# Moving the edge counting of a four-layer graph network into its two attention passes, the sort to the front, and the running maxima beside the dense products

## The reference, cut to what matters

```python
edge_index = jnp.stack([src, dst])
x = _layernorm(x + _L0_gnn_ref(x, edge_index, edge_attr, ...))  # MLP on [x[src], edge_attr], mean by dst
x = _layernorm(x + _L1_gnn_ref(x, edge_index, ...))             # two attention convolutions, 4 heads, then 1
x = _layernorm(x + _L2_gnn_ref(x, src, dst, ...))               # three SAGE convolutions
x = _layernorm(x + _L3_gnn_ref(x, edge_attr, ..., src, dst))    # softmax over edges by dst of x[src] + edge_attr

def sage_conv(h, Ws, Wn, b):                                    # _L2
    agg = segment_sum(h[src], dst, n)
    return h @ Ws + (agg * inv_deg) @ Wn + b

m = node_feats[src] + edge_feats                                # _L3
mx = segment_max(m, dst, n)
ex = exp(m - mx[dst]); a = ex / segment_sum(ex, dst, n)[dst]
agg = segment_sum(m * a, dst, n)
```

## Time and profile before

| | us |
|---|---|
| median of 3 runs (lowest to highest) | 3654.17 (3653.41 to 3660.13) |
| the profiled execution | 3656.58 |
| its span on the core | 3654.7 |
| PE, DVE, ACT, POOL busy | 2391.6, 2257.3, 1621.9, 1622.4 |
| granted PE clock, mean over the span | 0.781 |

### The profile page before, as it was taken

The page is one execution under the profiler, slowest core; times in us unless marked ns, Lnnn a source line. Parts: engine busy times, 40 slices in busy tenths (PEclk is TensorE's granted clock), DMA queues, the critical chain, the costliest instruction groups (busy, mean ns, idle before and its releaser), DMA issues.

```text
span 3654.7 us, 44760 instructions
## 1 busy us (share of the span) xinstructions
PE 2391.6 (65%) x9865; PEld 1648.7 (45%) x9865; DVE 2257.3 (62%) x6047; ACT 1621.9 (44%) x3304; POOL 1622.4 (44%) x1620
## 2 busy tenths in 40 slices
PE   6777778344444423444453777789999995666666
PEld 4665665234444323344342333335544543555554
DVE  5888885567777756787667666621111226666668
ACT  2887886334433232433322666633211234444443
POOL 4777760477777357777730000000000004777770
PEclk9999999655555555555556999989999997888886
DMA  6555550577777266777710545453321334555550
GB/s 205 154 160 155 161 143 11 140 194 201 205 198 203 51 169 176 201 196 206 198 36 14 163 162 164 161 157 92 98 72 45 108 117 112 148 148 151 150 147 26
DMA packets 675621, 511.58 MB, mean 140 GB/s; under 512 B 66405, under 2 KB 641758, under 8 KB 675024
## 3 DMA queue, kind: packets, MB, share of 16 engines
q1 hardware_dynamic: 614422, 370.87, 34.6%
q0 software_dynamic: 57904, 132.57, 14.5%
q10 hardware_dynamic: 3052, 5.38, 0.5%
HBM read 385.39 MB, written 123.19 MB: 139 GB/s over the span
## 4 chain that ended last, share of the span: by engine, by line
PE 28%; POOL 27%; DVE 16%; issue 14%; SPq 8%; DMA 3%; DVEq 2%; ACT 1%; POOLq 0%; ACTq 0%
POOL big L725 16%; PE ps L1116 15%; POOL y_and_h L739 11%; SPq L649 6%; PE ps L856 5%; DVE y_and_h L1589 3%; DVE big L1561 3%; DVE ps L1581 2%; PE ps L792 1%; SPq L644 1%; DMA big<-table_gat,big 1%; PE ps L778 1%; DVEq L494 1%; PE ps L955 1%; DVE w_sb L1759 1%
## 5 line engine op out<-in xcount | busy, mean ns | idle before, releaser
L725 POOL DMA_INDIRECT big<-table_gat,big x832 | 854.3, 1027 | 480.8 <-issue 247.8
L739 POOL DMA_INDIRECT y_and_h<-table_pool,src_block x391 | 396.5, 1014 | 1309.6 <-DMA table_pool<-x_sb 1190.7
L1561 DVE TENSOR_TENSOR big<-big,ps 128x257 f32 (+3 forms) x1664 | 590.8, 355 | 226.3 <-issue 22.4
L955 PE MATMUL ps<-y_and_h,work 128*128 128x136 f32 (+1 forms) x1664 | 437.0, 443 | 413.1 <-DVE y_and_h L1840 393.1
L955 PEld LDWEIGHTS ps<-y_and_h,work 128*128 128x128 f32 x1664 | 373.6, 325 | 443.1 <-DVE y_and_h L1840 442.9
L712 POOL DMA_INDIRECT big<-table_mlp,src_block x391 | 370.9, 948 | 158.8 <-issue 117.6
L1304 ACT ACTIVATE work<-iota,dst_rel 128x128 f32<-128x128 f32 x936 | 296.0, 387 | 68.8 <-PE ps L955 68.8
L1326 ACT ACTIVATE y_and_h<-y_and_h 128x128 f32<-128x128 f32 (+1 forms) x26 | 8.0, 309 | 670.9 <-DVE y_and_h L1817 670.9
L1367 ACT ACTIVATE work<-ps 128x800 uint16<-128x800 f32 x298 | 244.5, 836 | 136.3 <-DMA adjacency<-work 84.3
L856 PE MATMUL ps<-w_sb,work 128*128 128x256 f32 x832 | 210.9, 398 | 127.7 <-DVE y_and_h L1589 116.9
L1147 PE MATMUL ps<-big,y_and_h 128*128 x624 | 203.1, 483 | 129.5 <-DVE big L2210 128.3
(11 more groups left out here) (349 smaller groups left out, 4394.9 us busy)
## 6 DMA issues: line engine op xcount, KB each, us to landing
adjacency<-work SPq DMA_DIRECT2D x598, 100.0 KB, 1.7
work<-adjacency SPq DMA_DIRECT2D x9, 3200.0 KB, 11.9
big<-adjacency SPq DMA_DIRECT2D x9, 3200.0 KB, 11.9
work<-in_ea_blocks SPq DMA_DIRECT2D x416, 64.0 KB
work<-rel_rows SPq DMA_DIRECT2D x208, 128.0 KB
w_sb<-in_ea_blocks SPq DMA_DIRECT2D x97, 256.0 KB, 3.0
w_sb<-border_dram SPq DMA_DIRECT2D x194, 128.0 KB, 3.9
prefix_blocks<-w_sb SPq DMA_DIRECT2D x97, 256.0 KB
```

The lines of the kernel that those rows point to most:

```text
L725: pool.indirect_dma_start(ring[:, step % GAT_RING, :], None, table[k], bass.IndirectOffsetOnAxis(src_idx[:, step:step + 1], 0))\
L739: pool.indirect_dma_start(pool_rows[q][:, i, :], None, table["pool"], bass.IndirectOffsetOnAxis(src_block[:, block:block + 1], 0)).then_in ...
L955: mm = pe.matmul(sums_bank(g, j, width), onehot_of(k, g)[:, j, :], weighted[:, g % 2, j, 0:width], start=True, stop=True)
L1561: dve.tensor_tensor(to, to, bank_of(j), ALU.add).then_inc(accumulated, 1)
```

## The change

It moves four pieces of work.

1. **Sorting goes first.** `find_slots("pool")`, `ints_to_floats`, `split_sources`, `find_below`, `sort_into_windows` and PE's `place_windows` run before the MLP pass, on the edge list that is in SBUF there anyway. The keys are kept in `work` and copied to `xT` before gat1. PE's MLP products and POOL's first gather wait for `KEYS_KEPT`, ACT's zeroing of the sums for `EDGES_MOVED`. `place_steps` runs right before the gat1 pass.
2. **Counting goes into both attention passes.** All 299 pairs of steps are spread evenly over 416 places, two for each group: on DVE `mark_pairs(..., 0)` stands ahead of `add_sums` and `weigh`, `mark_pairs(..., 1)` behind `mark_nodes`. PE counts a pair one group later, into banks 6 and 7; ACT copies the pair (`read_pairs`); SP stores it three groups later. It is one forward chain; the join is gone, and with it the second pair of banks. PE starts a pair when ACT has copied the one before it (`pair_read`).
3. **The banks of the passes move.** The sums of the passes go to banks 2 to 5. The turned weights go to bank 1 and ACT copies them to SBUF (`copy_weights` into `weight_cols`), so `weigh` reads both operands from SBUF.
4. **Sweeps go beside the SAGE products.** On DVE they stand between the conversions, in proportion to the products' work (`sweeps_after`: 5.9 for a chunk of sage0 or sage2, 11.8 for one of sage1); SP's `move_sweeps` stands in the list between two loads of counts. There are four load buffers in place of two. A chunk has 384 columns now (`WIDTHS = [384] * 8 + [128]`, nine chunks for each convolution, 2400 KB). The first two chunks are loaded while layernorm 2 is made.

The core of the diff:

```diff
-WIDTHS = [512] * 6 + [128]
+WIDTHS = [384] * 8 + [128]
+HALF_SLOTS = 2 * len(GAT) * NG
+def pairs_at(n, q, part):
+    u = 2 * (n * NG + q) + part
+    return [p for p in range(PAIRS) if p * HALF_SLOTS // PAIRS == u] if 0 <= q < NG else []
...
+            def move_sweeps(n):
...
+                if n in (0, NBG):
+                    load_sweep(n)
+                    load_sweep(n + 1)
+                if n + 2 < (NBG if n < NBG else SWEEPS):
+                    load_sweep(n + 2)
+                if n % NBG >= 2:
+                    store_sweep(n - 2)
...
                     load_rows_of(rel_rows, rel_b, rel_loaded, g, g % 2)
-                    if g < NBG:
-                        load_sweep(n * NBG + g)
-                    if 2 <= g < NBG + 2:
-                        store_sweep(n * NBG + g - 2)
+                    store_pairs(pairs_at(n, g - 3, 0) + pairs_at(n, g - 3, 1))
...
                 for k, c, n in chunks():
+                    for part in range(HIGH // 2):
+                        for v in sweeps_after(n, part, HIGH // 2):
+                            move_sweeps(v)
+                    if n + 2 < 3 * NCHUNK:
+                        for by in range(2):
+                            sp.wait_ge(slice_ready[by], converted(n + 1, by))
+                        load_chunk(n + 2)
...
             pool.wait_ge(src_loaded, 16)
+            pool.wait_ge(windows_by_dve, KEYS_KEPT)
             gather_blocks("mlp", pre_ready, 0, LAG)
...
             pe.wait_ge(read_by["dve"], fills_read(FIRST_FILL["flag"], "dve"))
+            place_windows()
+            pe.wait_ge(windows_by_dve, KEYS_KEPT)
             for g in range(NG + 2):
...
+            def count_pairs(pairs):
+                if pairs and pairs[0] == 0:
+                    pe.wait_ge(windows_by_dve, BUILD_READY)
+                for p in pairs:
...
+                    if p:
+                        pe.wait_ge(pair_read, p)
+                    for i in range(2):
+                        step = 2 * p + i
+                        pe.wait_ge(cells_marked, step + 1)
+                        pe.wait_ge(lows_marked, step + 1)
+                        pe.matmul(cells(banks[i]), nothing, cell_no, start=True, stop=False, skip_group_check=True)
+                        mm = pe.matmul(cells(banks[2 + i]), low_marks[:, step % KEYS, :], cell_marks[step % KEYS],
+                                       start=False, stop=False, skip_group_check=True)
+                    mm.then_inc(pair_built, 1)
...
+                    count_pairs(pairs_at(n, q - 1, 0))
                     if q >= WEIGH:
                         sum_weighted(q - WEIGH)
-            def place_windows():
...
+                    count_pairs(pairs_at(n, q - 1, 1))
...
+                def copy_weights(x):
+                    act.wait_ge(weights_turned, batch_at + x + 1)
+                    if x >= 2:
+                        act.wait_ge(weighed, n * NG + (x - 1) * BATCH)
+                    act.activation(weight_cols[:, x % 2, 0:2 * R], ps[:, 1, P:P + 2 * R], ACT.Copy).then_inc(weights_copied, 1)
...
-                    both = ps[:, 2 + x % 2, 0:2 * R]
+                    both = weight_cols[:, x % 2, 0:2 * R]
...
+                    mark_pairs(pairs_at(n, q, 0))
                     if q >= ADD:
                         add_sums(q - ADD)
                     if WEIGH <= q < NG + WEIGH:
                         weigh(q - WEIGH)
                     if q + 1 < NG:
                         mark_nodes(q + 1)
-                    if q < NBG:
-                        sweep(n * NBG + q)
+                    mark_pairs(pairs_at(n, q, 1))
...
             for k, c, n in chunks():
                 for hi in range(1, HIGH, 2):
                     convert(n, hi)
...
+                    for v in sweeps_after(n, hi // 2, HIGH // 2):
+                        sweep(v)
```

More of the change, by code:

```diff
@@ L119, with staged_before, sweeps_after @@
 SUMMED_ON_DVE = ["mlp", "gat1", "gat2", "pool"]
[L122 to L129, removed]
+HALF_SLOTS = 2 * len(GAT) * NG
+def pairs_at(n, q, part):
+    u = 2 * (n * NG + q) + part
+    return [p for p in range(PAIRS) if p * HALF_SLOTS // PAIRS == u] if 0 <= q < NG else []
+def staged_before(p):
+    return 32 * (p // STAGED)
+SWEEP_WORK = [WIDTHS[c] * (2 if k == "sage1" else 1) for k in LAYERS for c in range(NCHUNK)]
+def sweeps_after(n, part, parts):
+    done = sum(SWEEP_WORK[:n]) * parts + SWEEP_WORK[n] * part
+    ends = [SWEEPS * at // (sum(SWEEP_WORK) * parts) for at in (done, done + SWEEP_WORK[n])]
+    return range(*ends)
 def ring_counts():
@@ L317, in program @@
[L317 to L330, removed]
+        chunk_no = part_of_big(15366, NCH)
@@ L610, in store_sweep, with store_pairs @@
                   .then_inc(sweep_stored[n % 2], 16)
+            def move_sweeps(n):
+                if n == 0:
+                    sp.wait_ge(borders_stored, 32)
+                    sp.wait_ge(swept, 1)
+                if n == NBG:
+                    for last in range(NBG - 2, NBG):
+                        store_sweep(last)
+                    for b in range(2):
+                        sp.wait_ge(sweep_stored[b], 16 * (NBG // 2))
+                if n in (0, NBG):
[5 more added lines that the diff above has]
+                    store_sweep(n - 2)
+            def store_pairs(pairs):
+                if pairs and pairs[0] == 0:
+                    sp.wait_ge(windows_by_dve, BUILD_READY)
+                for p in pairs:
+                    places = nc.values_load_multi_w_load_instructions(
+                        place_i[0:1, 2 * p:2 * p + 2], engines=(mybir.EngineType.SP,), min_val=0, max_val=NW + BUILD - 1,
+                        skip_runtime_bounds_check_because="the merge path, counted on the chip, stays in the grid")[1]
+                    sp.wait_ge(pair_read, p + 1)
+                    for odd in range(2):
+                        sp.dma_start(adjacency[bass.ds(places[odd], 1), :, :].rearrange("o p e -> p (o e)"),
+                                     staged[:, p % STAGED, odd, :]).then_inc(staged_out[p % STAGED], 16)
             def attention_rows(k):
@@ L652, in load_counts @@
[L652 to L660 removed]
+                    store_pairs(pairs_at(n, g - 3, 0) + pairs_at(n, g - 3, 1))
+                for g in range(NG, NG + 3):
+                    store_pairs(pairs_at(n, g - 3, 0) + pairs_at(n, g - 3, 1))
@@ L904, in _, with cells @@
             row_products("h1", 3, D + 2 * HEADS, [(xT, gcat["gat1"][:, :])], None)
+            def cells(bank):
+                return ps[:, bass.ds(bank, 1), 0:CELLS].rearrange("p o e -> p (o e)")
+            def count_pairs(pairs):
+                if pairs and pairs[0] == 0:
+                    pe.wait_ge(windows_by_dve, BUILD_READY)
+                for p in pairs:
+                    banks = nc.values_load_multi_w_load_instructions(
+                        bank_i[0:1, 4 * p:4 * p + 4], engines=(mybir.EngineType.PE,), min_val=BUILD_BANK, max_val=BUILD_BANK + 1,
+                        skip_runtime_bounds_check_because="a bank is found from a parity")[1]
+                    if p:
[8 more added lines that the diff above has]
+                    mm.then_inc(pair_built, 1)
             def attention_pass(k):
@@ L1571, in _ @@
             mean = sum_rows("mlp")
+            find_slots("mlp")
+            find_slots("pool")
+            sort_into_windows()
             link(dve.memset(elus[:, :, :, 256:257], 1.0))
-            find_slots("mlp")
             def add_node_terms(g):
@@ L1857, in attention_pass @@
                 for q in range(NG + ADD):
-                    if k == "gat2" and q in SORTING:
-                        SORTING[q]()
                     for later, stage in stages.items():
```

500 lines of the change are left out of this document (229 added, 271 removed).

## The result

The changed kernel takes 3492.1 us (median of 4 runs, 3490.8 to 3494.7) against 3654.5; the ratio is 0.9554, 95% interval 0.9537 to 0.957. It is 162 us faster. 300 were forecast, and the range ended at 3490. The profiled execution's span is 3492.9 us.

The account below looks back on a forecast made before the run. Attention passes were taken as bound by POOL's gathers, SAGE products by PE, with serial work behind gat2. 3656.6 - 451 + 59 - 39 + 0 + 130 = 3355.6, stated as 3355 us; range 3230 to 3490.

Parts of the forecast that it names:

- Behind gat2: Between gat2 and the SAGE products: all but layernorm and inverses goes, first loads of counts hidden under layernorm; -451 us.
- The front: Before and in the MLP pass: sorting delays POOL's first gather to about 109 us, then POOL sets the pace; +59 us.
- Scans out, weighing from SBUF in: Attention passes: gathers shorten by 66 us without scans, lengthen by 27 beside weighings, marks stretch nothing; sum -39 us.
- rival D: Attention passes: the added marks hold gathers back, +38 us, 3393 us in all; chance 0.05.
- Is POOL still the bound?: Attention passes: POOL needs 41.0 us a batch, DVE 36 and PE 34 stay below it; 0 us, at worst 26.
- Sweeps beside the products: SAGE stage: ordered transfers, a load of counts ahead of sweep loads and stores, delay DVE's conversions and PE; +130 us.
- A: SAGE stage: four load buffers let SP work ahead, so only transfer volume counts; 3257 us in all; chance 0.17.
- B: Attention passes: PE waiting for ACT's copy of each pair lengthens 26 batches by 130 us; 3485 us; chance 0.12.
- C: Attention passes: PE, ACT and DVE take turns instead of overlapping, 8.3 us a group; about 4020 us; chance 0.04.

Follow-up runs that it names:

- the two causes are taken out: Changed kernel with ACT writing each step's four head weights side by side and SP loading helper rows ahead of mask loads: gat1 567.3 us, whole 3450.2 us.

## Why the prediction was wrong, point by point

- **Behind gat2: right.** -453 us for -451; the loads of counts are hidden by the layernorm.
- **The front: right.** +60 for +59. The keys were kept at 108.5 us, and the pass then took POOL's pace, 391 gathers from 108.5 to 597.6 us. The additions that the forecast read at 541.09 are the first that need the last gathers; they stand at 601.75 now, where about 600 were forecast. Six more groups follow them in both kernels, to 571.1 and 631.4 us.
- **Scans out, weighing from SBUF in: right in gat2** (-19), and in gat1 too once the two causes are taken out (567.3 against the 563 that follow from the forecast). The gathers that start beside weighings are longer by 39 us in all, 12 in gat2 and 27 in gat1; the forecast had 27 for both passes, 38 at most. Those beside counting marks are longer by 12, which the forecast put at nothing. So the gathers of both passes gave back 13 us instead of 39. The Trainium skill ("SBUF — State Buffer", "SBUF: two separate sides") says that a DVE instruction in a two-port mode, or with two SBUF inputs, can hold the ports that it shares with GpSimd for its whole length. The trace agrees for the weighing, as at 1004.21 us, and for some of the marks; together the marks cost a third of the 38 us that rival D gave them. The row on one mark was a fair guide and not exact.
- **"Is POOL still the bound?": failed for gat1.** The step gave DVE 36 of 41 us a batch, with the weighing at its old 0.68 us. It priced what a second SBUF operand does to the gathers and forgot what it does to the instruction itself. With four heads the weights of one step lie 128 bytes apart; read that way from SBUF the weighing takes 1.035 us, 37 us more over the pass, and holds the gathers beside it for longer. That is the first half: from first to last gather gat1 takes 554.1 us, where 528 follow from the forecast (547.9 less half of 39), so 26 of the 48 us. The list of SP, put at 0, was the second half: its helper rows, late by 52 us in sum before, were covered by waits for gathers, and now they keep DVE back. DVE lags 56.2 us behind the last gather where it lagged 34.4, the other 22 us. `place_steps` may have spent some of the 5 us a batch too, which was not tried apart: the first weighing stands 67.6 us behind the first gather, 56.1 before. This lag then grew to 88 us within gat1, to 68 before.
- **Sweeps beside the products: mechanism right, size off.** The ordered chain was taken and not volume, and the runs show it. The first sweep that a load of counts holds up starts 11.8 us after the load's issue (median of 22; 11.2 forecast). The other step was taken as 2.55 us and is 3.36, beyond the upper end of 3.0: it left out that SP issues 384 KB of loads ahead of the store, so that the store is late and lands only after 4.1 us. These 172 steps come to 578 us, where the forecast had 177 steps and 451 us. The 23 steps behind a load come to 273 us (24 and 281), and the rest of the stage is 6 us, where the forecast had about 34 for the short chunks. (The prediction says that a store waits for the sweep after its own. It waits for its own alone; what delays it are the loads ahead of it.)
- **Rivals.** A (the order hides) fell: PE waited 168 us. B fell: PE waited 33 us in gat1 for ACT's copies of pairs, while removing DVE's and SP's causes brought the pass back to POOL's pace. PE also had more room than was forecast: the clock was to stay at 0.50 in the passes and was 0.69 and 0.73. C fell: the passes overlap. D was worth 12 of its 38 us.
- **The range.** It ended at the time of B alone. That two terms of the forecast could miss on the same side, gat1's and SAGE's, was not in it: SAGE's own upper end, +76, with nothing in gat1, gave 3431.

What stays open: how much of gat1's last 4 us is the late start, which was not tried apart; whether a third result buffer would do as much as the store's place; and whether the 57 us that PE is busy longer in SAGE, at the lower granted clock, lengthened the stage or only filled waits. With the sweeps left out both the waits and the longer products are gone (631 of 633 us busy, clock 1.00).

## What to carry to other kernels

Price a change of operand by the instruction that reads it as well as by its neighbours, and look at the stride: a longer instruction holds its neighbours for longer too. A wait that costs nothing is someone's cover: add up the waits that hide behind the bound before work is put on the engine that has them, since two of them became cost here as soon as DVE's room was gone. Where a queue works in order, put the transfer that frees a buffer ahead of those that fill one, and give a bulk load a queue of its own; here that was worth 179 us with no byte less to move.

## What the runs showed of the hardware

- A DVE product of 128x512 f32 whose second operand is four words 128 bytes apart, each set repeated 32 times, takes 1.035 us from SBUF, 0.679 from PSUM and 0.690 from SBUF when the four words are neighbours.
- A gather that POOL issues while DVE runs a product with both operands in SBUF is held: 81 gathers of gat1 started beside a weighing of 1.035 us and lasted 1.28 us on the mean, the longest 1.85, against 0.945 alone. Beside bf16 marks of 0.25 to 0.36 us 222 gathers lasted 1.00 us on the mean.
- While 2400 KB wait on a queue, the next issue on it can hold SP for 4.4 us instead of 0.37.
- The 16 DMA engines reached a share of 0.92 (267 GB/s) in a stage of 696 us with transfers from two queues; one queue with the same transfers stood at 0.75, and with the store first at 0.85 over 2014 to 2430 us.
- PE's granted clock in the attention passes rose from 0.50 to 0.69 and 0.73, between its two levels, when PE was busy 344 instead of 243 us in gat1. PE's sums (L955, now L1047) fell from 443 to 371 ns on the mean.
